# A fused attention and expert layer: the vector engine's work in step zero is written out in another order, and six more and six new idle transposes stand at the start

## What is computed

```
xn = layernorm(x)
q, k, v = xn @ Wq, xn @ Wk, xn @ Wv
alpha = sigmoid((xn @ Wg + bg) / 16)                 # one decay per token and head
state = alpha_t * state + k_t v_t ;  out_t = q_t state
att = (out * sigmoid(xn @ Wog)) @ Wo
scores = sigmoid(xn @ gate_w.T)                      # 64 experts in 8 groups
groups ranked by their two best, the best 4 kept, the 8 best experts of these kept,
weights = their scores / their sum * 2.5
ffn = each token's experts (silu(g) * u) @ w_down, weighted and added
result = x + att + ffn
```

## Time and profile before

| | us |
|---|---|
| median of 3 runs | 1276.55 (1276.54 to 1277.82) |
| the profiled execution | 1277.6 |
| its span on the core | 1275.8 |
| PE busy in the span | 1253.5 (98%) |
| DVE busy in the span | 935.7 (73%) |

### The profile page before, as it was taken

The page is one execution under the profiler, slowest core; times in us unless marked ns, Lnnn a source line. Parts: engine busy times, 40 slices in busy tenths (PEclk is TensorE's granted clock), DMA queues, the critical chain, the costliest instruction groups (busy, mean ns, idle before and its releaser), DMA issues.

```text
span 1275.8 us, 27850 instructions
## 1 busy us (share of the span) xinstructions
PE 1253.5 (98%) x9702; PEld 1108.0 (87%) x9702; DVE 935.7 (73%) x2215; ACT 575.7 (45%) x1171; POOL 486.1 (38%) x377
## 2 busy tenths in 40 slices
PE   7999999999999999999999999999999999999999
PEld 6788888888888888898898888988988899889887
DVE  6997878889797559867578586675785866757834
ACT  6565655656564444433344333333443343334422
POOL 2110011011001016437557375474574754745620
PEclk9999999999999999999999999999999999999999
DMA  6567535355342322257487475674874756747665
GB/s 237 166 234 216 174 108 169 121 174 170 121 153 76 101 78 89 88 137 189 109 191 172 120 170 132 160 189 103 188 171 118 170 135 156 188 106 186 157 194 185
DMA packets 124918, 194.66 MB, mean 153 GB/s; under 512 B 12016, under 2 KB 98608, under 8 KB 124592
## 3 DMA queue, kind: packets, MB, share of 16 engines
q1 hardware_dynamic: 94384, 147.99, 35.9%
q0 software_dynamic: 30464, 45.83, 19.9%
HBM read 148.62 MB, written 57.74 MB: 162 GB/s over the span
## 4 chain that ended last, share of the span: by engine, by line
PE 84%; DVE 11%; issue 2%; DMA 1%; ACT 1%; DVEq 0%; SPq 0%; ACTq 0%
PE bank L785 24%; PE bank L837 7%; PE bank L942 7%; PE bank L910 7%; PE bank L800 7%; PE bank L817 6%; PE bank L952 4%; PE bank L855 4%; PE bank L858 4%; PE bank L828 3%; PE bank L882 3%; PE bank L932 2%; DVE Dt L1485 2%; PE bank L894 2%; PE bank L870 2%
## 5 line engine op out<-in xcount | busy, mean ns | idle before, releaser
L627 POOL DMA_INDIRECT acc<-arena,idx_all x128 | 215.1, 1681 | 141.8 <-issue 74.5
L619 POOL DMA_INDIRECT arena<-table,idx_all x132 | 170.5, 1292 | 167.5 <-ACT share L1162 113.5
L785 PE MATMUL bank<-xp,wq 128*128 128x512 f32 x768 | 214.9, 415 | 0.0
L785 PE MATMUL bank<-xp,wk 128*128 128x512 f32 x768 | 202.3, 398 | 0.2 <-DVE wk L1395 0.2
L785 PEld LDWEIGHTS bank<-xp,wk 128*128 128x128 f32 x768 | 141.8, 188 | 34.0 <-DVE wk L1395 0.6
L785 PEld LDWEIGHTS bank<-xp,wq 128*128 128x128 f32 x768 | 141.0, 190 | 28.0 <-issue 0.5
L1485 DVE TENSOR_TENSOR_SCAN Dt<-decay,eye_b 128x512 f32<-128x512 f32 x128 | 157.2, 1230 | 0.0
L837 PE MATMUL bank<-qT,kT 128*128 128x128 f32 x1024 | 135.5, 275 | 1.8 <-DVE At L1506 1.8
L1138 ACT ACTIVATE qT<-bank 128x512 f32<-128x512 f32 x128 | 76.5, 598 | 130.9 <-PE bank L785 128.8
L837 PEld LDWEIGHTS bank<-qT,kT 128*128 128x128 f32 x1024 | 125.1, 192 | 2.7 <-DVE At L1506 2.1
L1138 ACT ACTIVATE kT<-bank 128x512 f32<-128x512 f32 x128 | 76.4, 597 | 99.1 <-PE bank L785 98.6
(11 more groups left out here) (172 smaller groups left out, 2235.8 us busy)
## 6 DMA issues: line engine op xcount, KB each, us to landing
decay<-decay_dram SPq DMA_DIRECT2D x64, 512.0 KB, 5.1
carry<-decay_dram SPq DMA_DIRECT2D x60, 512.0 KB
arena<-in_L_attn_x_dram SPq DMA_DIRECT2D x16, 512.0 KB, 4.6
table<-arena SPq DMA_DIRECT2D x16, 512.0 KB, 3.7
xT_dram<-arena SPq DMA_DIRECT2D x16, 512.0 KB, 3.0
arena<-in_L_ffn_w_gate_dram SPq DMA_DIRECT2D x64, 128.0 KB
arena<-in_L_ffn_w_up_dram SPq DMA_DIRECT2D x64, 128.0 KB
arena<-in_L_ffn_w_down_dram SPq DMA_DIRECT2D x64, 128.0 KB, 3.8
```

Of the source, the lines that this page charges most:

```text
L619: pool.indirect_dma_start(out=xg[:, e % 2, j, :], out_offset=None, in_=table[:, :], in_offset=bass.IndirectOffsetOnAxis(ap=idx_all[:, e, j ...
L627: pool.indirect_dma_start(out=acc[:, :], out_offset=bass.IndirectOffsetOnAxis(ap=idx_all[:, e, j:j + 1], axis=0), in_=yb[:, e % 2, j, :], ...
L785: last = mm(to[:, :], w[:, part, k, h * DK:(h + 1) * DK], xp[:, other, k, :], start=(k + i == 0), stop=(k == KD - 1 and i == 2))
```

## The change

On DVE: `gates(0)` goes ahead of the low part of Wq. The scans (0, 2) and (0, 3) and the low part of Wo leave the prologue. The first decayed scores, At of head 0, then stand right behind the scans (0, 0) and (0, 1); ranks, top and weights of chunk 0 and the gates of chunk 1 follow at place 1 of s = 1, and only then At of head 1. In step 0 a table of its own, `first_scans`, takes the place of `scan_ahead`: two scans at s = 2, one at 3 and 4, two at 5, none at 6, three at 7, one at 8; the low part of Wo stands at s = 3. On PE: 24 idle transposes of the identity instead of 18 at the start, 6 new ones ahead of the first router; and the first router no longer waits for ACT's high copies of the tokens (`xT_cp`), only for DVE's copies (`xT_dve`) and for the router's weights.

```diff
-PE_WARM = 18
+PE_WARM = (24, 6)
...
-            for _ in range(PE_WARM):
+            for _ in range(PE_WARM[0]):
                 tr(bank[5][:, 0:P], ident[:, :], ident[:, :])
...
             def router(c):
-                pe.wait_ge(xT_cp, 2 * (c + 1))
                 if is_first(c):
                     pe.wait_ge(xT_dve, 2)
                     pe.wait_ge(gwT_cp, 1)
+                else:
+                    pe.wait_ge(xT_cp, 2 * (c + 1))
...
             tokens_back(0, 1)
+            for _ in range(PE_WARM[1]):
+                tr(bank[5][:, 0:P], ident[:, :], ident[:, :])
             router(0)
...
             dve.wait_ge(w_const, 64)
+            gates(0)
             weights_low("q")
-            gates(0)
             decays_products(0)
...
+            def first_scans(s):
+
+                for c, h in {2: ((0, 2), (0, 3)), 3: ((0, 4),), 4: ((0, 5),), 5: ((0, 6), (0, 7)),
+                             7: ((1, 0), (1, 1), (1, 2)), 8: ((1, 3),)}.get(s, ()):
+                    decay_scan(c, h)
+                if s == 3:
+                    weights_low("o")
...
-                    if (s, place) in ((0, 4), (3, 3), (6, 3)):
+                    if (s, place) in ((0, 4), (3, 3), (6, 3)) and not (is_first(c) and s == 0):
                         route_ranks(n - 1)
                         route_top(n - 1)
+                    if is_first(c) and (s, place) == (1, 1):
+                        route_ranks(0)
+                        route_top(0)
                     if s % 3 == 1 and place == 1:
                         route_weights(n - 1)
-                    if (s, place) in ((1, 3), (4, 3), (H, 1)):
+                    if (s, place) in ((1, 1) if is_first(c) else (1, 3), (4, 3), (H, 1)):
                         gates(n)
...
-                    scan_ahead(c, s)
+                    if is_first(c):
+                        first_scans(s)
+                    else:
+                        scan_ahead(c, s)
...
             decay_scan(0, 0)
             decay_scan(0, 1)
-            weights_low("o")
-            decay_scan(0, 2)
-            decay_scan(0, 3)
             step(0, "norm")
```

## The result

| | before | changed |
|---|---|---|
| median (us) | 1276.63 (1276.54 to 1277.82, 5 runs) | 1282.62 (1281.59 to 1284.67, 5 runs) |
| the profiled execution | 1277.6 | 1283.09 |
| its span | 1275.8 | 1281.3 |

The ratio is 1.0044, its 95% interval 1.003 to 1.0058: slower by 6.0 us. The direction was the forecast one, the size was not: 2.4 us were forecast, and the time lies above the range's 1281.6.

A forecast was written before the change was run, and what follows sets the result against it. DVE's work in step 0 was taken to decide when step 1 begins: front -1.2, old waits -1.8, new waits +1.2, x of chunk 2 +4.2, together +2.4 us on 1276.55, forecast 1279.0 us, range 1275.4 to 1281.6.

The forecast's parts named there:

- What bounds the first 90 us: Step 0: DVE's last work decides when step 1 begins (88.24 us before); PE's stall of 1.84 us lies off the chain.
- The front: Start of step 0: gates come earlier, so DVE's low part of Wk and all behind it start 1.2 us earlier.
- the transposes are no help to the clock: PE's start: idle transposes don't raise its clock; the tokens' transposes stay at 0.23 us each, the router ends at 16.0.
- this moves the sum by less than 0.1 us: Front: whether or not idle transposes raise PE's clock, gates precede ACT's 16.97, so the sum moves under 0.1 us.
- x of chunk 2 +4.2: DVE's statistics of chunk 2, step 0: the load of x lands 9.43 us after the fourth scan; DVE waits 4.2 us.
- the upper bound of 5.8: DVE's wait for x of chunk 2: at most 5.8 us, with the longest load, 5.4 us, after the same store.
- PE starts again on a low clock. That costs nothing more: PE, stopped from about 48 until 52: its low clock afterwards adds nothing, as DVE needs its next product at 59.
- old waits gone -1.8: DVE in step 0: its two earlier waits, 1.1 us for ACT and 0.7 for PE, disappear.
- new short waits +1.2: DVE in step 0: 0.6 and 0.4 us for ACT and 0.2 ahead of At of head 1, 1.2 in all.
- slower still: Rival, 26%: PE's clock falls again around 87 to 91 (+1.5), x of chunk 2 lands late (+1.6); 1280.5, both 1282.

The follow-up runs named there:

- scans_late: Changed kernel with SP's decay load behind chunk 1's traffic and step 0's scans of chunk 1 spread, two behind the tokens' low part: 1277.31 us, ratio 0.999.
- front_only: Kernel before with only the front's edits (idle transposes, router's dropped wait, gates ahead of the low part of Wq): 1277.31 us, ratio 0.9995.
- sp_order: Changed kernel with SP's load of the decays of heads 6 and 7 in step 0 moved behind chunk 1's traffic: 1278.48 us, ratio 1.0006.
- scans_late_warm: scans_late plus twelve idle transposes on PE ahead of the outputs of the last pair of heads in step 0: 1276.32 us, ratio 0.9983.
- sp_order_before: Kernel before with only SP's decay load in step 0 moved behind chunk 1's traffic: 1278.06 us, ratio 1.0001.
- changed_again: Changed kernel run once more, unaltered, for a second profile: 1284.02 us, ratio 1.0052.
- warm_18: Changed kernel with 18 idle transposes at the start and none ahead of the router: 1286.36 us, timed only once.
- changed_no_warm: Changed kernel without any idle transpose: 1285.15 us, ratio 1.0046.
- dec_late: Changed kernel with GpSimd's stores of the decays of chunk 1 held until x of chunk 2 has landed: 1284.93 us, ratio 1.0047.
- changed_warm_late: Changed kernel with twelve idle transposes filling PE's stop for At of head 7 in step 0: 1282.72 us, ratio 1.0034.
- scans_first: Changed kernel with the third and fourth scan one place earlier, right behind the first At: 1278.86 us, ratio 1.0012.
- sp_order_warm: sp_order plus twelve idle transposes filling PE's stop for At of head 7 in step 0: 1277.63 us, ratio 0.9994.

## Why the prediction was wrong

**(a) What bounds the first 90 us: right.** DVE sets the start of step 1 after the change too: the first product, at 93.84, follows the tokens' low part (92.25 + 1.47) by 0.12 us, and taking scans away from in front of it moves it (scans_late). That PE's stall and its slow clock at 40 us lay off the chain held too: from the first scans to step 1 took 59.3 us with the stall (before, front_only) and without it (sp_order).

**(b) The front: right, with an accident on top.** -1.2 was forecast. The low part of Wk starts at 18.28 instead of 20.56, and the first scan at 26.77 instead of 28.90, 2.1 us. The gates' path was read rightly: ACT's table load ended before the sigmoids, and nothing waited for the gates. But that load itself began at 14.65, where I had held it at 15.69, because Wq, for which ACT waits ahead of it in both kernels, had landed by 12.72 and not by 13.76. That us is not the change's doing. In scans_late_warm, with the same front, Wq had landed by 13.70, nearly as before, and the low part of Wk started so:

```profile
19.26 2.29 DVE L1404 TENSOR_TENSOR wk<-Dt,wk 128x2048 fp32r<-128x2048 f32 x1 [0.44 <-ACT wk L1120]
```

20.56 - 19.26 is 1.3 us: the term was sized well, and luck with Wq made the measured execution 1 us quicker than it had to be. What I had not seen is that the front can lose its gain ahead of the first scans: their decays landed too late for it in six of the profiles, by 0.2 to 0.6 us in four and by 1.3 and 1.5 us in sp_order and scans_late.

That the transposes are no help to the clock was wrong: **the row of before showed one execution, not the rule**. The kernel before and sp_order_before have the same 18 transposes and the same start on PE; their eight token transposes took 1.97 us in one profile and, here, 1.09 (timeline of PE, sp_order_before):

```profile
3.26 4.10 PE L690 MATMUL bank<-ident 128*128 128x128 f32 x18 [3.26 <-POOL arena L562]
...
8.87 1.09 PE L707 MATMUL bank<-ident,arena 128*128 128x128 f32 x8 [0.21 <-ACT arena L1076]
12.05 3.69 PE L717 MATMUL bank<-arena 128*128 128x72 f32 x16 [2.09 <-ACT xp L1096]
```

The Trainium skill's "TensorE: Matmul & The Clock Gate", Part 4, by which the fast clock doesn't engage for transposes, disagrees with these rows; Part 1, that activity releases the throttle, agrees. I had held that this moves the sum by less than 0.1 us; with Wq early it moved the low part of Wk by 0.7 us (18.28 and 19.00 without the transposes).

**(c) The wait for x of chunk 2: the mechanism right, the size too small. This is the step that failed: the term "x of chunk 2 +4.2".** The forecast's chain holds link by link: fourth scan at 39.31 (forecast 39.65), SP's decay load on its heels, the store at 39.70, the load when the store had landed, and DVE waiting. The term "+4.2" measured 7.62 us in the first profile, and 4.88, 5.58, 6.3, 6.6 and 6.77 in the other five of this order: the middle is 6.5, and the upper bound of 5.8 was below four of the six. Two things went into it:
- DVE asked 4.75 us after the fourth scan (44.06) and not 5.2. This half us lengthens the wait and costs nothing, since the landing decides. Nor does the front's gain come back as wait: the scan that releases the transfer is DVE's own, so an earlier DVE brings the landing forward with it, and -1.2 and the wait do add.
- From the scan's end to the landing took 12.35 us instead of 9.43. The store took 7.35 instead of 5.2 and the load 4.5 instead of 3.8. This is the 2.9 us that cost time. The view by stretches, changed kernel (PE, its loads, DVE, ACT, POOL; clock, DMA share, GB/s), shows how:

```profile
44.00:45.00 1.00, 1.00 (x6) 0.82 (x5) 0.07 (x1) 1.00 (x5) 0.00 (x0) 1.00 1.01 405
45.00:46.00 1.00, 1.00 (x6) 0.82 (x5) 0.00 (x0) 0.98 (x3) 0.00 (x0) 1.00 0.36 128
46.00:47.00 1.00, 1.00 (x10) 0.90 (x8) 0.00 (x0) 0.95 (x1) 0.00 (x0) 1.00 0.07 27
47.00:48.00 1.00, 0.08 (x1) 0.00 (x0) 0.00 (x0) 0.00 (x0) 0.00 (x0) 1.00 0.06 23
```

From 46 to 48 the sixteen DMA engines moved 25 GB/s with a mean busy share of 0.06 to 0.07, which is about one of sixteen. I read this as one engine still at its part of the two stores (to `table` and of the transpose), with the rest done; no view here shows the engines one by one. In changed_again the store had landed at 45.6, at 332 GB/s, and the thin stretch (49 GB/s, 46 to 47) came behind it. Why the tail is there, and why only where this store follows the scan late, is open: holding GpSimd's stores back left 6.2 us. It landed in 5.1 to 5.3 us in the eight profiles in which DVE doesn't wait for it, and in 5.2 (twice), 6.2, 7.2, 7.3 and 7.4 in the six in which DVE does.

The Trainium skill's "DMA: Bandwidth & Descriptors", Anatomy of one DMA, whose fit gives 3.2 us for 512 KB, states it for single transfers on GpSimd's path, and these are SyncE's and queue behind each other; it is further off here than it was against before: in no profile did this store land in under 5.1 us, nor this load in under 3.6.

**(d) The other waits, and the clock.** From the landing to the first product of step 1 took 42.16 us (51.68 to 93.84), against 41.5 forecast. It is tempting to put these 0.7 us on PE's long stop and the low clock behind it (the four transposes of line 831 there took 1.12 us). sp_order refutes that: without the late load, and at full clock, the same stretch took 42.15 (45.47 to 87.62). "PE starts again on a low clock. That costs nothing more" was right. What was wrong are the terms "old waits gone -1.8, new short waits +1.2": together they came to 0.0 in sp_order and +0.1 in the changed kernel (67.07 us from the first scans to step 1, less the wait of 7.62, is 59.45, against 59.34 before), not to -0.6.

The rival **slower still** is what happened: its first part (PE's clock falls again behind its stop at 87 to 91) in changed_again, warm_18, changed_no_warm and dec_late, its second (a landing at the upper bound or past it) in changed, changed_warm_late, warm_18 and changed_no_warm. It gave 1280.5 to 1282 for these, with 26%; the median of 1282.62 lies above even that. Over all fourteen profiles the first part reads so: where PE stands still for 1.4 us or more for At of head 7 (seven kernels: changed, changed_again, warm_18, changed_no_warm, dec_late, sp_order, scans_first), PE ran at 0.50 between 85 and 99 us in five; where it doesn't (before, front_only, sp_order_before, sp_order_warm, scans_late, scans_late_warm, changed_warm_late), in none. It costs 1.9 to 2.4 us where it happens: from the outputs behind that stop (line 858 of the changed kernel) to the first product of line 913 were 8.9 us in the changed kernel and in sp_order, 11.3 in changed_again, scans_first and dec_late, and 10.8 in warm_18 and changed_no_warm. I had priced it at 1.5, and left it out of the sum. The stop is there in sp_order and scans_first too, so the change's order of scans brings it and not the late load.

So the sum of the profiled execution, in the prediction's terms, reads: front -2.1 (forecast -1.2), short waits +0.1 (-0.6), x of chunk 2 +7.6 (+4.2), together +5.6 (+2.4), which is 93.84 against 88.24. In changed_again: -1.5, +0.1 and +4.9, together +3.5, and +2.4 for the clock. Of the changed kernel's 6 us 4 to 5 are the late load (sp_order takes 1.0044 to 1.0006, scans_first to 1.0012). The rest, 1 to 2, stays open: the clock behind the stop is a part that the profiles show and the medians only lean to (changed_warm_late 1.0034, sp_order_warm 0.9994).

**The version that beats both.** scans_late_warm: the changed kernel with SP's load behind the traffic of chunk 1, the scans of chunk 1 spread with two behind the tokens, and the stop filled. Its gain over before, 2.0 us, is small, but its interval leaves out 1; that over scans_late (0.9983 and 0.999) can't be told, and in the profile the transposes cost it 1.2 us at the start of step 1, so which part brings the last 0.7 stays open.

## What to carry to other kernels

When an instruction is moved on one engine, follow the semaphore that it sets into every queue that waits for it, and list all that stands behind the waiter there: here one scan moved by 5 us carried a store and a load on which nobody had waited before. A landing on which nobody waited is a weak measure for the same transfer once the path depends on it: the one row read 5.2 us for the store, and in the six profiles with the wait it was 5.2 to 7.4. Then ask, for a gain ahead of a wait, whether the thing waited for comes forward with it. The load of x did, since the engine's own scan released it; the decays of chunk 0 came forward by less, and took up to 1.5 us of the front's gain. To compare two orders, time the stretch between two marks that both have: 59.3 us before and after said at once that the new order by itself was worth nothing. And read a clock or a stall that shows in one profile as one draw: a second profile of the same program showed the same time made up of other parts.

## What was not expected of the hardware

- Idle transposes of an identity can raise PE's clock: eight transposes took 1.09 to 1.13 us behind 24 of them (ten profiles) and behind 18 (two of three), and 1.97 in the third of these, that of before, and with none ahead of them (one profile).
- The view's granted clock for the first microseconds doesn't fit the durations. For the kernel without idle transposes it prints 1.00 where the products took twice their usual time:

```profile
8.00:11.00 3.00, 2.08 (x10) 1.57 (x8) 1.28 (x4) 2.29 (x5) 0.00 (x0) 1.00 1.04 421
```

  The duration of a known product tells the level there.
- A stop of PE of 1.4 to 1.5 us was followed by half the clock in five of seven profiles, and not in the other two, with the same program among both (changed and changed_again). Behind stops of 1.8 and 2.2 us (the three profiles with the old order of scans) and of 5.4 to 7.5 us (the six with the late load) it always was.
- A store of 512 KB landed 2 us late, with a tail of 2 us in which only 25 GB/s were moved at a busy share of 0.06 to 0.07, about that of one DMA engine of sixteen; beside it only the store of the transpose was still under way.
